# DLRM tower on one Trainium2 core: two tables' last rows fetched by SyncE, high parts of tables placed in PSUM, casts ahead, and another order of a group's work

## The chip, the cores and the metric

The kernel runs on one core of one Trainium2 chip. The time is the device time of that core in microseconds (us), the median of several runs. PE is the matrix engine (TensorE), DVE VectorE, ACT ScalarE, POOL GpSimd, SP SyncE; a q behind a name is that engine's sequencer. The span of a profile runs from the first instruction to the last, and the device time of the same execution is a little longer.

## The reference

For 2048 samples, 26 ids each pick one 128-wide row of 26 tables (nine of those with 1000 rows are called hot tables here; the other 17 have 1000 to 125000 rows). With the sample's dense row these are 27 vectors; their 351 pairwise dot products and the dense row go through a three-layer MLP.

```python
e = jnp.stack([tbl_0[ids[:, 0]], ..., tbl_25[ids[:, 25]]], axis=1)
combined = jnp.concatenate([dense[:, None, :], e], axis=1)           # 2048 x 27 x 128
inter = jnp.einsum('bnd,bmd->bnm', combined, combined)[:, triu_i, triu_j]
h = jnp.concatenate([dense, inter, dense], axis=1)                    # 607 wide
h = jnp.maximum(h @ W_top1 + b_top1, 0.0)                             # 512
h = jnp.maximum(h @ W_top2 + b_top2, 0.0)                             # 256
y = h @ W_top3                                                        # 1
```

## The kernel before

The batch is cut into 16 tiles of 128 samples; two tiles are a group (8 groups). Work is written as a list of steps per tile, and PE, ACT and DVE each walk the same list and do their own part of each step, in order. The lists are `FIRST_STEPS` (before group 0), `STEPS` (two lists, for the first and second tile of groups 0 to 6) and `LAST_STEPS` (group 7). A letter and a number are one step:

- Q, transposes: PE transposes the gathered rows of one bank of 3 or 4 tables of the **next** tile (L650) into `transpose_ps`; ACT (even n, L408) or DVE (odd n, L545) copies them to `embed_t`.
- H, look-up in a hot table for the **next** group: DVE makes a one-hot matrix of the ids (L538, reads ids that PE has broadcast into PSUM at L659, once for two look-ups), PE multiplies it with the table's high and low part (L684, 16 products), ACT copies the result (L461). Each one-hot is made two look-ups ahead, as soon as its slot of two is free. Even n use the bank `hot_ps`, odd n bank 1 of `mlp_ps`.
- G, gram: PE forms the dot products of 64 samples (L714, 128 records); ACT copies the late columns (L455), then DVE the early ones (L527, COPY_PREDICATED) into `units`.
- SP then stores a group's `units` to DRAM (`bounce`, L316), waits, and reads them back in another layout (L320). S of the **following** group is the split of what landed: ACT casts the high part (L449), DVE subtracts for the low part (L549).
- M0 to M3, M4 and M5, M6: the three layers of the MLP for the **previous** group (L720 to L722, 12 products each, and L761). M0 needs the low part of S. ACT applies the activation (L416, L420), DVE takes the low part (L569); M2 uses the bank of M0, and waits for M0's low part.
- D splits the group's dense rows (ACT L442, DVE L549); E copies dense rows into `embed_t`. W splits the MLP weights in group 0 alone.

POOL does one thing: 272 indirect gathers, 17 a tile (L390), each waiting that the same bank of two tiles earlier has been transposed. SP issues all other transfers from one queue, in order. Its loop over the groups is

```python
for g in range(GROUPS - 1):
    if g + 2 < GROUPS:
        load_dense(g + 2)          # waits for D of group g: its buffer is dense_sb[g % 2]
    pack(g, g % 2, packed_raw)     # bounce and read back
    if g >= 1:
        store_y(g - 1)
```

In the start, nine hot tables are loaded, ACT casts each to `table_hi` (L488, fp32r), and DVE subtracts this from the loaded table for `table_lo` (`split_lo`, L549).

Of the kernel before, what the change touches and what calls it, by code (L numbers as in the profile page):

```python
# [41 lines left out]
P = 128  # L42
TABLES = 26
N = TABLES + 1
B = 2048
# [22 lines left out]
PAIR_ROWS = HOT * GROUPS // PAIR  # L68
HALF = N // 2
# [27 lines left out]
    "G0 S0 Q0 H0 M0 Q1 Q2 H1 G1 W0 Q3 H2 W1 M1 Q4 M2 W2 H3 W3".split(),  # L97
    "G0 M3 Q0 H4 W4 M4 D0 E0 Q1 Q2 H5 W5 G1 Q3 H6 M5 Q4 H7 H8 M6".split(),
# [13 lines left out]
def dlrm_tower(nc, dense_t, ids, hot_ids, row_numbers, tables, w1_dense, w1_again, w1_units, b1, w2, b2, w3, identity, late_rows, bounce, y):  # L112
    ctx = ExitStack()
    with ctx:
# [24 lines left out]
        selector = sb("selector", [P, PAIR_ROWS], F32R)  # L139
# [14 lines left out]
        y_sb = sb("y_sb", [P, 2, GROUP], F32)  # L154

        def unit_p(c):

            return BIAS_P if c == 0 else UNIT_P

# [17 lines left out]
        stage_b = y_sb[:, :, :].rearrange("p i b -> p (i b)")  # L177
# [20 lines left out]
        selector_ready = sem("selector_ready")  # L198
        hot_ids_ready = sem("hot_ids_ready")
# [3 lines left out]
        banks_zeroed = sem("banks_zeroed")  # L203
# [50 lines left out]
        def dense_columns(g):  # L254

            return dense_group(g).rearrange("p (q s) -> p s q", s=BLOCK)

# [34 lines left out]
        def _(sp):  # L292
# [30 lines left out]
            def store_y(g):  # L323

                sp.wait_ge(mlp_copied, MLP_USES * (g + 1) + (g < GROUPS - 1))
                sp.dma_start(y[g * GROUP:(g + 1) * GROUP, :].rearrange("b c -> c b"), y_sb[0:1, g % 2, :]).then_inc(y_stored[g % 2], 16)
# [49 lines left out]
        def _(pool):  # L376
            def gather(tile):
# [6 lines left out]
                for u in range(TILE_BANKS):  # L384
# [3 lines left out]
                    for f in features(u):  # L388
                        table = GATHERED_TABLES[f - 1]
# [5 lines left out]
            nc.gpsimd.dma_start(hot_ids_sb[:, :], hot_ids).then_inc(hot_ids_loaded, 16)  # L395
# [8 lines left out]
        def _(act):  # L404
# [5 lines left out]
            def mlp_copy(g, buf, m):  # L410
# [6 lines left out]
                elif m < H1_CHUNKS + H2_CHUNKS:  # L417

                    c = m - H1_CHUNKS
                    nc.scalar.activation(hidden2[c].rearrange("p (q s) -> p s q", s=BLOCK),  # L420
                                         src.rearrange("p (s q) -> p s q", s=BLOCK),
                                         ACT.Relu, bias=b2_sb[:, c:c + 1]).then_inc(mlp_copied, 1)
                else:
                    if g >= 2:

                        act.wait_ge(y_stored[g % 2], 16 * (g // 2))
                    nc.scalar.copy(y_sb[0:1, g % 2, :], src[0:1, :]).then_inc(mlp_copied, 1)
# [93 lines left out]
        def _(dve):  # L521
# [78 lines left out]
            nc.vector.memset(gram_ps[:, :, :], 0.0).then_inc(banks_zeroed, 1)  # L600

            dve.wait_ge(const_loaded, 16 * 2)
            nc.vector.tensor_copy(selector[:, :], identity_sb[:, 0:PAIR_ROWS]).then_inc(selector_ready, 1)
# [32 lines left out]
        def _(pe):  # L636
# [4 lines left out]
            def transposes(g, buf, t2, u):  # L641
                tile = TILES * g + t2
                pe.wait_ge(gathered[t2][u], 16 * len(features(u)) * (g + 1))
# [5 lines left out]
                for i, f in enumerate(features(u)):  # L649
                    last = nc.tensor.transpose(transpose_ps[:, (t2 * TILE_BANKS + u) % 2, i, :], rows[:, t2, f - 1, :], identity_sb[:, :])  # L650
                last.then_inc(transposed, 1)

            def broadcast_ids(pair):

                if pair >= 1:
# [4 lines left out]
                                 selector[:, pair:pair + 1].to_broadcast([P, HOT_P]), hot_ids_sb[:, :],  # L660
                                 start=True, stop=True).then_inc(hot_ids_ready, 1)

# [165 lines left out]
            pe.wait_ge(hot_ids_loaded, 16)  # L828
            broadcast_ids(0)

# [79 lines left out]
```

## Time and profile before

| | us |
|---|---|
| median of 3 runs (381.84 to 385.08) | 384.82 |
| the profiled execution | 385.81 |
| its span | 383.9 |
| PE busy | 333.5 |
| POOL busy | 269.4 |
| DVE busy | 260.9 |
| ACT busy | 169.3 |

The busy time of POOL leaves out 0.30 us between two gathers, in which its sequencer issues the next one; the engine does nothing else in that time.

### The profile page before, as it was taken

The numbers are of one execution on the slowest core, as the hardware profiler recorded it, in microseconds if no ns is written. First come the engines' busy times: TensorE is split into PE (matmuls) and PEld (weight loads), VectorE is DVE, ScalarE is ACT, GpSimd is POOL, SyncE is SP. The second block draws the span as 40 slices with busy tenths as digits, with TensorE's granted clock in tenths as the row PEclk, the third lists the DMA queues.
The fourth block names the chain that finished last, engine by engine and source line by source line (L and its number), as shares of the span: only waits on it lengthen the run. The fifth ranks groups of instructions, "written<-read, shape, count | busy, mean of one in ns | idle before, by whom it ended". The sixth has DMA issues, their size and how long they took to land.

```text
span 383.9 us, 13545 instructions
## 1 busy us (share of the span) xinstructions
PE 333.5 (87%) x6208; PEld 303.5 (79%) x6208; DVE 260.9 (68%) x206; ACT 169.3 (44%) x248; POOL 269.4 (70%) x277
## 2 busy tenths in 40 slices
PE   3777895949899998999899989999898989969787
PEld 2656784939898897979898879889897889859676
DVE  3999889574849865787668775777666776723322
ACT  2553563514445443545364543544354434532412
POOL 6787777777777777777777777777777777776000
PEclk9999998797999999999999999999999999997999
DMA  7996124251224322242215221341224112332020
GB/s 181 234 236 188 51 70 112 57 158 50 56 55 118 88 58 56 66 144 52 56 51 158 51 57 54 94 121 50 56 66 143 51 50 58 97 99 56 2 92 0
DMA packets 18985, 33.51 MB, mean 87 GB/s; under 512 B 5834, under 2 KB 11666, under 8 KB 18930
## 3 DMA queue, kind: packets, MB, share of 16 engines
q0 software_dynamic: 8848, 18.11, 18.2%
q1 hardware_dynamic: 10082, 14.55, 13.5%
q8 instruction: 49, 0.80, 0.8%
q14 instruction: 6, 0.05, 0.0%
HBM read 28.96 MB, written 3.68 MB: 85 GB/s over the span
## 4 chain that ended last, share of the span: by engine, by line
PE 40%; POOL 34%; issue 13%; DVE 7%; DMA 3%; ACT 2%; DVEq 0%; SPq 0%
POOL rows L390 34%; PE gram_ps L714 8%; PE hot_ps L684 8%; PE mlp_ps L684 8%; PE mlp_ps L720 4%; DVE one_hot L538 3%; PE transpose_ps L650 3%; PE mlp_ps L721 3%; PE mlp_ps L722 3%; DVE units L527 2%; DMA rows<-table,ids_sb 1%; PE hot_ids_ps L659 1%; PE mlp_ps L761 1%; DMA rows<-bounce 1%; DVE packed_lo L549 1%
## 5 line engine op out<-in xcount | busy, mean ns | idle before, releaser
L390 POOL DMA_INDIRECT rows<-table,ids_sb x272 | 268.5, 987 | 83.5 <-issue 80.7
L538 DVE TENSOR_TENSOR one_hot<-hot_ids_ps,row_numbers_sb 125x2048 fp32r<-125x2048 f32 x72 | 165.2, 2298 | 72.2 <-PE hot_ids_ps L659 62.7
L684 PE MATMUL hot_ps<-one_hot,table_hi 125*128 125x256 f32 x320 | 82.5, 295 | 3.4 <-issue 2.9
L684 PE MATMUL hot_ps<-one_hot,table_lo 125*128 125x256 f32 x320 | 79.6, 286 | 0.0
L684 PE MATMUL mlp_ps<-one_hot,table_hi 125*128 125x256 f32 x256 | 66.6, 297 | 11.8 <-DVE hidden_lo L569 6.4
L684 PEld LDWEIGHTS hot_ps<-one_hot,table_hi 125*128 125x128 f32 x320 | 62.1, 194 | 4.6 <-issue 4.6
L714 PE MATMUL gram_ps<-embed_t 128*27 128x27 f32 x4096 | 54.9, 195 | 11.2 <-issue 4.8
L684 PE MATMUL mlp_ps<-one_hot,table_lo 125*128 125x256 f32 x256 | 63.8, 286 | 0.0
L714 PEld LDWEIGHTS gram_ps<-embed_t 128*27 128x27 f32 x4096 | 45.0, 106 | 23.0 <-issue 15.4
L684 PEld LDWEIGHTS hot_ps<-one_hot,table_lo 125*128 125x128 f32 x320 | 62.3, 195 | 0.1
L684 PEld LDWEIGHTS mlp_ps<-one_hot,table_hi 125*128 125x128 f32 x256 | 49.9, 195 | 14.6 <-DVE one_hot L538 7.4
L408 ACT COPY embed_t<-transpose_ps 128x512 f32<-128x512 f32 (+1 forms) x48 | 55.1, 1148 | 7.8 <-PE transpose_ps L650 7.6
L461 ACT COPY embed_t<-hot_ps 128x256 f32<-128x256 f32 x40 | 27.3, 683 | 53.6 <-PE hot_ps L684 53.6
L527 DVE COPY_PREDICATED units<-late_sb,gram_ps 128x208 f32<-128x208 int32 x32 | 35.2, 1101 | 22.2 <-ACT units L455 22.1
L650 PE MATMUL transpose_ps<-identity_sb,rows 128*128 128x128 f32 x272 | 43.3, 282 | 7.9 <-DMA rows<-table,ids_sb 7.9
L684 PEld LDWEIGHTS mlp_ps<-one_hot,table_lo 125*128 125x128 f32 x256 | 50.0, 195 | 0.0
L650 PEld LDWEIGHTS transpose_ps<-identity_sb,rows 128*128 128x128 f32 x272 | 31.9, 143 | 12.1 <-DMA rows<-table,ids_sb 9.8
L455 ACT COPY units<-gram_ps 128x224 f32<-128x224 f32 x32 | 17.9, 561 | 51.7 <-PE gram_ps L714 51.7
L461 ACT COPY embed_t<-mlp_ps 128x256 f32<-128x256 f32 x32 | 21.8, 682 | 36.7 <-PE mlp_ps L684 36.5
L545 DVE COPY embed_t<-transpose_ps 128x384 f32<-128x384 f32 x32 | 33.0, 1032 | 0.0
L720 PE MATMUL mlp_ps<-packed_hi,w1u_hi 126*128 126x256 f32 (+1 forms) x90 | 26.4, 294 | 3.8 <-DVE packed_lo L549 3.8
L721 PE MATMUL mlp_ps<-packed_lo,w1u_hi 126*128 126x256 f32 (+1 forms) x90 | 25.8, 286 | 0.0
(80 smaller groups left out, 381.4 us busy)
## 6 DMA issues: line engine op xcount, KB each, us to landing
rows<-table,ids_sb POOLq DMA_INDIRECT x272
embed_t<-table SPq DMA_DIRECT2D x8, 448.0 KB
bounce<-units SPq DMA_DIRECT2D x8, 448.0 KB, 2.6
scratch<-bounce SPq DMA_DIRECT2D x7, 378.0 KB
dense_sb<-dense_t SPq DMA_DIRECT2D x8, 128.0 KB
scratch<-w SPq DMA_DIRECT2D x1, 512.0 KB, 4.8
units<-w_units SPq DMA_DIRECT2D x2, 252.0 KB
scratch<-table SPq DMA_DIRECT2D x1, 448.0 KB
```

The source lines that it names most:

```text
L390: nc.gpsimd.indirect_dma_start(rows[:, t2, f - 1, :], None, tables[table], bass.IndirectOffsetOnAxis(ids_sb[:, tile, table:table + 1], 0)) ...
L408: nc.scalar.copy(embed_target(g, t2, u), embed_source(t2, u)).then_inc(even_copied, 1)
L455: nc.scalar.copy(unit_slot(buf, r, 0, UNITS), gram_slot(r, HALF, N)).then_inc(late_copied, 1)
L461: nc.scalar.copy(out, hot_bank(k).rearrange("p (t b) -> p t b", t=TILES)).then_inc(hot_copied, 1)
L527: nc.vector.copy_predicated(unit_slot(buf, r, 1, UNITS), rows_taken, gram_slot(r, 0, HALF)).then_inc(early_copied, 1)
L538: nc.vector.tensor_tensor(one_hot[:, k % RING], ids.to_broadcast([HOT_P, HOT_STEPS, GROUP]), row_numbers_sb[:, :, None].to_broadcast([HOT_ ...
L545: nc.vector.tensor_copy(embed_target(g, t2, u), embed_source(t2, u)).then_inc(odd_copied, 1)
L650: last = nc.tensor.transpose(transpose_ps[:, (t2 * TILE_BANKS + u) % 2, i, :], rows[:, t2, f - 1, :], identity_sb[:, :])
L684: last = nc.tensor.matmul(hot_bank(n), table[:, n, step, :], one_hot[:, k % RING, step, :], start=(step == 0 and table is table_hi), stop= ...
L714: last = nc.tensor.matmul(gram_ps[32 * s:32 * s + N, r % 2, q * N:(q + 1) * N], embed_t[:, slot, b, :], embed_t[:, slot, b, :], start=True ...
L720: nc.tensor.matmul(out, w[0], x[0], start=start, stop=False)
L721: nc.tensor.matmul(out, w[0], x[1], start=False, stop=False)
```

## The change

- **SP fetches rows.** The last two gathered tables of tile 15 are left out of POOL's gathers (270 instead of 272). SP reads their 256 ids into registers, 16 at a time, and issues one transfer of one row for each, in six portions (48, 48, 48, 48, 32, 32 rows) behind a group's `pack` and `store_y`. They land in `last_rows`, which takes the place of `y_sb`; y now leaves from row 0 of `hidden2_first`, and ACT waits for the store of y before it writes `hidden2_first` again.
- **High parts in PSUM.** PE multiplies `table_hi` with an identity into the two `gram_ps` banks (`place_hi`, two products of 512 columns), and `split_lo` reads the high part there instead of from SBUF. Each `place_hi` waits until the low part of the table before is done. The zeroing of `gram_ps` goes away, and the unused half of `hot_ids_sb` is zeroed by DVE instead of loaded.
- **Casts ahead.** ACT casts one hot table further ahead.
- **Order.** The two lists of `STEPS` are written anew. `FIRST_STEPS` and `LAST_STEPS` are as before.

```diff
 STEPS = [
-    "G0 S0 Q0 H0 M0 Q1 Q2 H1 G1 W0 Q3 H2 W1 M1 Q4 M2 W2 H3 W3".split(),
-    "G0 M3 Q0 H4 W4 M4 D0 E0 Q1 Q2 H5 W5 G1 Q3 H6 M5 Q4 H7 H8 M6".split(),
+    "G0 S0 Q0 H0 W0 H1 G1 Q1 W1 M0 M1 Q2 M2 H2 W2 Q3 H3 W3 Q4 M3 H4".split(),
+    "G0 Q0 H5 W4 M4 M5 G1 Q1 E0 Q2 H6 W5 H7 Q3 H8 Q4 D0 M6".split(),
 ]
...
+            def fetch_rows(loads):
+
+                for _ in range(loads):
+                    n, at = divmod(fetched["rows"], P)
+                    table = GATHERED_TABLES[GATHERED - SP_TABLES + n]
+                    with ExitStack() as held:
+                        numbers = [held.enter_context(sp.register(f"row{n}_{at + i}")) for i in range(SP_LOAD)]
+                        sp.load(numbers, last_ids[n:n + 1, at:at + SP_LOAD])
+                        for i, number in enumerate(numbers):
+                            row = sp.snap(number, min_val=0, max_val=ROWS[table] - 1)
+                            sp.dma_start(last_rows[at + i:at + i + 1, n, :], tables[table][bass.ds(row, 1), :]).then_inc(rows_fetched, 16)
+                    fetched["rows"] += SP_LOAD
...
                 if g >= 1:
                     store_y(g - 1)
+                if g < len(SP_LOADS):
+                    fetch_rows(SP_LOADS[g])
...
                     for f in features(u):
+                        if fetched_by_sp(tile, f):
+                            continue
...
             split_hi(0)
+            split_hi(1)
             for step, n in [(x[0], int(x[1:])) for x in FIRST_STEPS]:
                 if step == "H":
-                    if n + 1 < HOT:
-                        split_hi(n + 1)
+                    if n + 2 < HOT:
+                        split_hi(n + 2)
...
             def split_lo(k):
-                dve.wait_ge(hi_split, k + 1)
-                lower(raw_tables[k], table_hi[:, k], table_lo[:, k]).then_inc(lo_split, 1)
+                dve.wait_ge(hi_placed, k + 1)
+                nc.vector.tensor_tensor(in_banks(table_lo[:, k]), in_banks(raw_tables[k]), gram_ps[0:HOT_P, :, :],
+                                        ALU.subtract).then_inc(lo_split, 1)
...
+            def place_hi(k):
+
+
+                pe.wait_ge(hi_split, k + 1)
+                if k >= 1:
+
+                    pe.wait_ge(lo_split, k)
+                for a in range(2):
+                    last = nc.tensor.matmul(gram_ps[:, a, :], identity_r[0:HOT_P, :], in_banks(table_hi[:, k])[:, a, :],
+                                            start=True, stop=True)
+                last.then_inc(hi_placed, 1)
...
+            place_hi(0)
 
             for _ in range(FIRST_WARM_PRODUCTS):
...
                 if step == "H":
+                    if n + 1 < HOT:
+                        place_hi(n + 1)
                     look_up(0, n)
```

SP's queue around one `pack`, before: the stretch is one turn of the loop over the groups (g = 2). `dense_split_lo` is set by DVE's part of D, `early_copied` by DVE's part of the group's last G.

```order
L301 DMA dense_sb<-dense_t 128x256 [waits dense_split_lo,dense_placed]
L316 DMA bounce<-units 128x896 [waits early_copied]
L320 DMA scratch<-bounce 126x4x192 [waits units_stored]
L326 DMA y<-y_sb 1x256 [waits mlp_copied]
L301 DMA dense_sb<-dense_t 128x256 [waits dense_split_lo,dense_placed]
```

The same turn after the change, up to the first fetched row (47 more of them follow, with two more reads of ids):

```order
L315 DMA dense_sb<-dense_t 128x256 [waits dense_split_lo,dense_placed]
L330 DMA bounce<-units 128x896 [waits early_copied]
L334 DMA scratch<-bounce 126x4x192 [waits units_stored]
L340 DMA y<-hidden_first 1x256 [waits mlp_copied]
L351 TENSOR_LOAD last_ids_ptr
L351 REGISTER_ALU
L351 TENSOR_LOAD last_ids
L353 ISA
L354 DMA last_rows<-table 1x128
```

The order of the first three transfers is unchanged: the dense load, with its wait for D, stands ahead of the bounce.

DVE in the second tile of a group and into the next group, before, from D to the first low part of the MLP (COPY_PREDICATED is G, `dense_lo` is D, `packed_lo` is S, `hidden_lo` is the MLP's low part):

```order
L549 TENSOR_TENSOR dense_lo<-dense_sb,dense_hi 128x256 [waits dense_split_hi]
L545 COPY embed_t<-transpose_ps 128x3x128 [waits transposed]
L538 TENSOR_TENSOR one_hot<-hot_ids_ps,row_numbers_sb 125x2048 [waits hot_ids_ready,hot_ready]
L527 COPY_PREDICATED units<-late_sb,gram_ps 128x16x13 [waits late_copied]
L545 COPY embed_t<-transpose_ps 128x3x128 [waits transposed]
L538 TENSOR_TENSOR one_hot<-hot_ids_ps,row_numbers_sb 125x2048 [waits hot_ready]
L538 TENSOR_TENSOR one_hot<-hot_ids_ps,row_numbers_sb 125x2048 [waits hot_ids_ready,hot_ready]
L538 TENSOR_TENSOR one_hot<-hot_ids_ps,row_numbers_sb 125x2048 [waits hot_ready]
L527 COPY_PREDICATED units<-late_sb,gram_ps 128x16x13 [waits late_copied]
L549 TENSOR_TENSOR packed_lo<-scratch,packed_hi 126x768 [waits units_hi]
L538 TENSOR_TENSOR one_hot<-hot_ids_ps,row_numbers_sb 125x2048 [waits hot_ids_ready,hot_ready]
L569 SCALAR_TENSOR_TENSOR hidden_lo<-mlp_ps,hidden_hi 128x256 [waits mlp_copied]
```

The same boundary after the change:

```order
L573 TENSOR_TENSOR one_hot<-hot_ids_ps,row_numbers_sb 125x2048 [waits hot_ids_ready,hot_ready]
L584 TENSOR_TENSOR dense_lo<-dense_sb,dense_hi 128x256 [waits dense_split_hi]
L562 COPY_PREDICATED units<-late_sb,gram_ps 128x16x13 [waits late_copied]
L584 TENSOR_TENSOR packed_lo<-scratch,packed_hi 126x768 [waits units_hi]
L573 TENSOR_TENSOR one_hot<-hot_ids_ps,row_numbers_sb 125x2048 [waits hot_ready]
L573 TENSOR_TENSOR one_hot<-hot_ids_ps,row_numbers_sb 125x2048 [waits hot_ids_ready,hot_ready]
L562 COPY_PREDICATED units<-late_sb,gram_ps 128x16x13 [waits late_copied]
L580 COPY embed_t<-transpose_ps 128x3x128 [waits transposed]
L605 SCALAR_TENSOR_TENSOR hidden_lo<-mlp_ps,hidden_hi 128x256 [waits mlp_copied] x3
```

D has moved from the middle of the group's second tile to its end, next to S of the following group, and between S and the first `hidden_lo` there now stand two one-hots, a G and a copy where one one-hot stood.

## Rows read from the trace of the kernel before

**Rows 1.** The page: the span.

```profile
span 383.9 us, 13545 instructions
```

**Rows 2.** POOL's waits: releaser, total us, times, longest us.

```profile
POOL rows L390 <- issue: 80.7, 265, 0.3
```

**Rows 3.** Timeline of PE: start us, us, instruction [idle before].

```profile
83.02 1.25 PE L714 MATMUL gram_ps<-embed_t 128*27 128x27 f32 x103 [1.06 <-ACT embed_t L461]
...
128.63 1.91 PE L714 MATMUL gram_ps<-embed_t 128*27 128x27 f32 x128
...
212.14 1.88 PE L714 MATMUL gram_ps<-embed_t 128*27 128x27 f32 x128
...
334.09 0.66 PE L650 MATMUL transpose_ps<-identity_sb,rows 128*128 128x128 f32 x4 [0.50 <-DMA rows<-table,ids_sb]
...
339.74 1.73 PE L714 MATMUL gram_ps<-embed_t 128*27 128x27 f32 x118
```

**Rows 4.** PE's waits from 90 to 335 us.

```profile
PE mlp_ps L684 <- DVE hidden_lo L569: 6.4, 6, 1.3
PE transpose_ps L650 <- DMA rows<-table,ids_sb: 2.2, 4, 1.3
PE mlp_ps L684 <- ACT scratch L420: 1.8, 4, 0.6
```

**Rows 5.** Timeline of POOL and DVE around one table's low part, and the last gather.

```profile
12.83 1.21 DVE L549 TENSOR_TENSOR table_lo<-embed_t,table_hi 125x1024 fp32r<-125x1024 f32 x1
13.09 1.78 POOL L390 DMA_INDIRECT rows<-table,ids_sb  x1 [0.30 <-issue]
...
352.99 0.94 POOL L390 DMA_INDIRECT rows<-table,ids_sb  x1 [0.30 <-issue]
```

**Rows 6.** The chain that ended last: one look-up's 16 products.

```profile
336.76 1.92 PE hot_ps L684 x16
```

**Rows 7.** Timeline of SP and of the ACT cast behind the last pack.

```profile
200.54 0.36 SPq L301 DMA_DIRECT2D dense_sb<-dense_t  x1
204.47 0.34 SPq L316 DMA_DIRECT2D bounce<-units  x1
...
366.26 0.35 SPq L316 DMA_DIRECT2D bounce<-units  x1
...
372.19 1.02 ACT L515 CAST packed_hi<-rows 126x256 fp32r<-126x256 f32 x3 [6.50 <-DMA rows<-bounce]
```

**Rows 8.** Timeline of ACT, DVE and PE at a G, S and M0.

```profile
182.29 1.09 DVE L527 COPY_PREDICATED units<-late_sb,gram_ps 128x208 f32<-128x208 int32 x1
183.00 1.19 DVE L545 COPY embed_t<-transpose_ps 128x384 f32<-128x384 f32 x1
...
215.03 0.86 ACT L449 CAST packed_hi<-scratch 126x768 fp32r<-126x768 f32 x1
...
215.99 1.17 DVE L549 TENSOR_TENSOR packed_lo<-scratch,packed_hi 126x768 fp32r<-126x768 f32 x1
...
217.09 2.27 DVE L538 TENSOR_TENSOR one_hot<-hot_ids_ps,row_numbers_sb 125x2048 fp32r<-125x2048 f32 x1
...
217.22 0.39 PE L720 MATMUL mlp_ps<-packed_hi,w1u_hi 127*128 127x256 f32 x1 [0.47 <-DVE packed_lo L549]
...
218.40 0.93 PE L650 MATMUL transpose_ps<-identity_sb,rows 128*128 128x128 f32 x7
...
219.28 0.41 DVE L569 SCALAR_TENSOR_TENSOR hidden_lo<-mlp_ps,hidden_hi 128x256 fp32r<-128x256 f32 x1
```

**Rows 9.** Stretches: PE, PEld, DVE, ACT, POOL busy, granted clock, DMA.

```profile
344.40:351.20 6.80, 5.52 (x143) 5.03 (x144) 2.48 (x4) 1.54 (x3) 5.28 (x6) 0.50 0.22 58
```

**Rows 10.** Timeline of PE in group 7, where no pack is late.

```profile
342.84 0.27 PE L714 MATMUL gram_ps<-embed_t 128*27 128x27 f32 x10 [1.37 <-issue]
...
345.68 0.58 PE L720 MATMUL mlp_ps<-packed_hi,w1u_hi 127*128 127x256 f32 x1 [1.75 <-DVE packed_lo L549]
...
359.39 1.27 PE L714 MATMUL gram_ps<-embed_t 128*27 128x27 f32 x128 [1.37 <-ACT embed_t L408]
```

More of the change, by code:

```diff
@@ L68 @@
 PAIR_ROWS = HOT * GROUPS // PAIR
+HOT_IDS_P = 64
+SP_TABLES = 2
+SP_LOAD = 16
+SP_LOADS = [3, 3, 3, 3, 2, 2]
 HALF = N // 2
@@ L109, with dlrm_tower @@
 FIRST_STEPS = "H0 Q0 H1 Q1 H2 H3 Q2 H4 H5 Q3 H6 H7 Q4 E0 H8".split()
-def dlrm_tower(nc, dense_t, ids, hot_ids, row_numbers, tables, w1_dense, w1_again, w1_units, b1, w2, b2, w3, identity, late_rows, bounce, y):
+def dlrm_tower(nc, dense_t, ids, hot_ids, last_ids, row_numbers, tables, w1_dense, w1_again, w1_units, b1, w2, b2, w3, identity, late_rows, bounce, y):
     ctx = ExitStack()
@@ L153, in dlrm_tower, with fetched_by_sp @@
         hidden2_first = sb("hidden2_first", [P, GROUP], F32)
-        y_sb = sb("y_sb", [P, 2, GROUP], F32)
+        last_rows = sb("last_rows", [P, 2 * SP_TABLES, P], F32)
         def unit_p(c):
             return BIAS_P if c == 0 else UNIT_P
+        def fetched_by_sp(tile, f):
+            return tile == TILE_COUNT - 1 and f > GATHERED - SP_TABLES
         def by_chunk(at):
@@ L256, in dense_columns, with in_banks @@
             return dense_group(g).rearrange("p (q s) -> p s q", s=BLOCK)
+        def in_banks(table):
+            return table.rearrange("p (a j) d -> p a (j d)", a=2)
         def gram_slot(i, first, last):
@@ L419, in mlp_copy @@
                     c = m - H1_CHUNKS
+                    if c == 0 and g >= 1:
+                        act.wait_ge(y_stored[(g - 1) % 2], 16 * ((g + 1) // 2))
                     nc.scalar.activation(hidden2[c].rearrange("p (q s) -> p s q", s=BLOCK),
@@ L423, in mlp_copy @@
                 else:
[L424 to L427 removed]
+                    nc.scalar.copy(hidden2_first[0:1, :], src[0:1, :]).then_inc(mlp_copied, 1)
             def dense_place(g):
@@ L642, in transposes @@
                 tile = TILES * g + t2
-                pe.wait_ge(gathered[t2][u], 16 * len(features(u)) * (g + 1))
+                others = sum(fetched_by_sp(tile, f) for f in features(u))
+                pe.wait_ge(gathered[t2][u], 16 * (len(features(u)) * (g + 1) - others))
+                if others:
+                    pe.wait_ge(rows_fetched, 16 * SP_TABLES * P)
                 if u >= 2:
@@ L649, in transposes @@
                 for i, f in enumerate(features(u)):
-                    last = nc.tensor.transpose(transpose_ps[:, (t2 * TILE_BANKS + u) % 2, i, :], rows[:, t2, f - 1, :], identity_sb[:, :])
+                    source = last_rows[:, f - 1 - GATHERED + SP_TABLES, :] if fetched_by_sp(tile, f) else rows[:, t2, f - 1, :]
+                    last = nc.tensor.transpose(transpose_ps[:, (t2 * TILE_BANKS + u) % 2, i, :], source, identity_sb[:, :])
                 last.then_inc(transposed, 1)
@@ L890 @@
         late[:, k:k + HALF, k - 1] = 1
-    hot_ids = np.zeros((P, PAIR * GROUP), np.int32)
+    last_ids = np.ascontiguousarray(a["ids"][B - P:, GATHERED_TABLES[GATHERED - SP_TABLES:]].T)
+    hot_ids = np.zeros((HOT_IDS_P, PAIR * GROUP), np.int32)
     hot_ids[:PAIR_ROWS] = a["ids"].T[HOT_TABLES].reshape(HOT, GROUPS, GROUP).transpose(1, 0, 2).reshape(PAIR_ROWS, PAIR * GROUP)
```

25 lines of the change are left out of this document (14 added, 11 removed).

## Prediction

> **What bounds the kernel now.** I read POOL's waits first. In 265 of 272 gathers it waited for nothing but its own issue time, 0.30 us each [rows 2], so POOL runs without a stop from the start to its last gather at 352.99 us [rows 5]. The timeline of PE then tells how close PE runs behind it. Take the first G of each even tile as a mark: tile 2 at 83.02, tile 4 at 128.63, tile 8 at 212.14, tile 14 at 339.74 [rows 3]. Between tiles 4 and 8 a group takes (212.14 - 128.63) / 2 = 41.8 us. POOL needs 34 x 1.25 = 42.5 us for a group, plus lengthened gathers. So PE is the faster by a little, comes up to POOL late in the run, and waits for it there: the transposes at 334.09 waited for rows [rows 3], and over 90 to 335 us such waits sum to only 2.2 us [rows 4]. From the mark at 339.74 to the end of the span (383.9 [rows 1]) are 44.2 us of PE work and of the last pack. Two chains nearly tied: a gain on POOL counts only if PE can follow.
>
> **Gathers left to SP.** Two gathers fewer end POOL 2.5 us sooner in tile 15. It helps nothing by itself: the last bank of tile 15 was transposed behind queued MLP products, just before the G at 359.39 [rows 10], and the last rows had landed by about 355.5 (352.99 plus the 2.5 us from issue to landing that separates 331.59 from 334.09). SP pays. One transfer costs its queue 0.34 to 0.36 us with 128 partitions [rows 7]; taking that for one row, 48 rows are 17 us a group, and even 0.8 us each would be 38, inside a group. The transfers stand behind pack and store_y, so what they could delay is the next turn's dense load, a group later. I take 0, and +5 us at worst. The reads of ids have no row. The Trainium skill ("DMA: Bandwidth & Descriptors", on hardware figures) has a floor of about 600 ns for a tensor_load; by that three reads would add 1.8 us to the 17, which changes nothing.
>
> **High parts in PSUM.** While DVE takes a table's low part from two SBUF operands (1.21 us at 12.83), the gather that overlaps it takes 1.78 us instead of 0.94 [rows 5]; the one-hots of 2.3 us, one operand in PSUM, lengthen none. There are eight lengthened gathers up to 40 us, five by 0.84 and three by 0.16 to 0.33: 5.0 us in all. With the high part read from PSUM I expect them gone and every gather from 40 us on 5.0 us earlier. The price is PE's: 18 products, and at the start `place_hi(0)` waits for ACT's cast and the eight warm-up products now stand behind it, so the first look-up and DVE's chain of one-hots start 2 us later. DVE bounds the start before and after, so group 0 begins 2 us later. The zeroing, the halved load of ids and the cast ahead lie off this chain: 0.
>
> **Group 0, new order.** PE has no MLP there. From tile 0's mark to tile 2's took 40.6 us before, of which 3.9 us were a wait for rows that now land 5 us earlier, and some 3 us a half clock behind it. DVE's list is about 28 us up to the last one-hot of the group, PE's own work about 31. I take 34 us from a start at 44.5: tile 2's mark at 78 instead of 83.0. Bounds: 76 and 82.
>
> **A middle group, new order.** What is removed: PE's waits of H3 behind M2 and of H7 behind M5, (6.4 + 1.8) / 5.9 groups = 1.4 us a group by idle time [rows 4], about 1.8 start to start. So a group without waits is 41.8 - 1.8 = 40.0 us. What is added comes from D. SP's dense load waits for D and stands ahead of the bounce. Before, D was in mid-tile, the load went out at 200.54 and the bounce at 204.47, when G was done, not D [rows 7]; the rows were back before the next group began. Now D is the last step but one. Let 0 be PE's first G of the next group. That G waits for ACT's copy of Q4, and ACT casts D right behind that copy, then DVE subtracts: D is done at +1.1, or at +2.0 in every second group, where DVE's one-hot ahead of D first needs an id broadcast. The bounce goes out 0.4 later, and from a bounce to ACT's start on the rows it reads back took 372.19 - 366.26 = 5.93 us [rows 7]; in mid-run, with gathers beside it, I take 6.2. ACT's S so starts at a = +7.7 (or +8.6).
>
> From there, start to start [rows 8]: DVE's S at a + 0.96, the next instruction 1.10 later, and M0's products on the landed rows at a + 2.2. DVE was blocked at S and must then make two one-hots (2.19 each, 217.09 to 219.28), G's copy (0.71, 182.29 to 183.00), Q1's copy (0.75 taken alike), and only then M0's low part (0.41), all of which stand ahead of it in its queue: done at a + 0.96 + 1.10 + 4.38 + 0.71 + 0.75 + 0.41 = a + 8.3. M2 writes over M0's bank and waits for it: +16.1, and +17.6 in the other groups, where the broadcast of the second one-hot's ids waits for the first (0.7 more). Without waits M2 would start at two G (1.9 each), two H (1.92 [rows 6]), Q0 to Q2 (1.0), M0 and M1 (1.4 each, nine products in 1.18 us [rows 8]) and a broadcast (0.2): +11.7. So this costs 4.4 or 5.9, mean 5.1 us. Smaller: G for Q4's copy 0.2, M3 for H3's copy 0.4, H8 right behind H7 0.2. A group is then 40.0 + 5.9 = 45.9 us, against 41.8. Its bounds: below, 42.9, if only M0's own lateness (1 to 2 us) counts and DVE's queue does not; above, 47.
>
> **The clock.** Three times the granted clock of PE fell to half for 6.8 us, as in 344.40 to 351.20 [rows 9] (the two levels are 1.2 and 2.4 GHz). Ahead of that one stood gaps of 1.37 and 1.75 us with a little work between [rows 10]; ahead of another a single gap of 3.9. The new order has in each of six groups a gap of 3 to 4 us and a shorter one. I expect a fall in four of the six, each worth 3.4 us less what of it lies in the gap, 2.4: 9.6 us. Bounds 0 and 17. The Trainium skill ("TensorE: Matmul & The Clock Gate", part 1) ties the low level to an idle stretch of PE; read strictly, gaps cut up by work would not bring it, and the result is the rival "no falls" below. The fall at 344.40 came behind a cut-up gap, so this trace leans the other way.
>
> **Sum.** Tile 2 at 78; six groups of 45.9 are 275.4 (the packs of groups 0 to 5 stand behind a dense load; that of group 6 does not, so the last group is as before): tile 14 at 353.4. Plus 44.2: 397.6. Plus 9.6: span 407.2. The profiled execution was 1.9 over its span (385.81), the median 384.82 0.9 over it; with 0.9: **408 us**, 6% slower. POOL, 5 us ahead, is no bound any more.
>
> **Rivals.** (1) No falls of the clock: 397.6 + 0.9 = 398.5. For it: group 0's idle pieces of 1 to 2 us bring none. (2) The other side: S's lateness does not reach PE, because the pack is quicker or D done sooner than I have it. Then POOL bounds: tile 14's last rows land at 334.05 - 5.0 = 329.05, the transposes take 0.4, ACT's copy 1.64 more before G (H7 and H8, 3.8 us, no longer stand between), tile 14's mark at 331.1 and the end at 375.3, device 376. It decides where a group stays under (331.1 - 78) / 6 = 42.2 us; the point of no change is (339.7 - 78) / 6 = 43.6. What speaks against it: it needs under 2.2 us of waits, and S alone lands at +7.7. (3) DVE's queue is not what M2 waits for, and a group is 42.9: mark at 335.4, then 380.5, device 381 to 386 with a fall or two: no change. (4) SP's rows take over 0.85 us each and push the dense load beyond D: 3 to 5 us more a group, 420 or over.
>
> **How the numbers follow.** Slower with falls 0.47, without 0.27, SP overrun 0.03; faster 0.17; no change 0.06. A difference of 1% is about what a measurement of this kernel can tell. Case (3) lies partly on either side of that bound, so: faster 0.18, same 0.08, slower 0.74. The slow cases' own range is 392 to 420. To leave out no more than 2 in 10 I cut off most of the faster case and the overrun: 384 to 422.
>
> **What would show it.** Marks of tile 2 at 76 to 82 and then 45 to 49 us apart; the bounce 0.4 us behind each dense load, both about 1 us into the next group; ACT's S at +7.7; DVE idle 4 to 5 us ahead of `packed_lo`; PE idle at M2 for `hidden_lo`; half clock in most middle groups; no gather lengthened before 40 us; POOL waiting for transposes late in the run, since PE falls behind it. I am wrong if `packed_lo` does not wait, or if M2 starts before +13.

## The result, and the profile after

The changed kernel took **415.86 us** (median of 4 runs, 411.40 to 419.58) against 384.73 us for the kernel before on the same chip. The ratio is 1.0781, 95% interval 1.0685 to 1.0877: 8% slower. Ratios here and below leave out runs in which the chip was in a slower state, so they are not quite the quotient of the medians beside them. The profiled execution took 417.02 us, 1.8 over its span.

The page of the changed kernel: the span, the granted clock of PE in 40 slices (9 is full speed), and the chain that ended last.

```profile
span 415.2 us, 14406 instructions
...
PEclk9999999997999779998999969999899969998989
...
PE 47%; DVE 31%; DMA 14%; ACT 4%; issue 3%; SPq 1%; DVEq 0%
```

POOL held 34% of the chain before and has no share of it now; DVE's one-hots and the two transfers of a pack have taken its place. The marks (PE's first G of an even tile, which answer to [rows 3]):

```profile
79.57 0.63 PE L767 MATMUL gram_ps<-embed_t 128*27 128x27 f32 x47 [1.48 <-ACT embed_t L441]
...
129.62 0.56 PE L767 MATMUL gram_ps<-embed_t 128*27 128x27 f32 x44 [0.16 <-ACT embed_t L441]
...
179.89 0.29 PE L767 MATMUL gram_ps<-embed_t 128*27 128x27 f32 x13 [0.37 <-ACT embed_t L441]
...
370.65 0.53 PE L767 MATMUL gram_ps<-embed_t 128*27 128x27 f32 x40 [0.37 <-ACT embed_t L441]
```

Three stretches hold the account: tile 2 is reached 3.5 us sooner than before, the six middle groups take (370.65 - 79.57) / 6 = 48.5 us each, and the end is 44.6 us long as it was (44.2). Stretches of the changed kernel (columns as in [rows 9]):

```profile
0.00:79.57 79.57, 62.15 (x888) 55.02 (x889) 68.04 (x49) 36.56 (x49) 59.35 (x66) 1.00 0.53 140
79.57:370.65 291.08, 248.97 (x4622) 229.41 (x4622) 180.04 (x137) 112.70 (x174) 200.01 (x210) 0.94 0.26 73
370.65:415.20 44.55, 34.34 (x717) 31.30 (x717) 13.26 (x21) 14.00 (x27) 0.00 (x0) 0.92 0.06 21
```

and the same middle stretch of the kernel before:

```profile
83.02:339.74 256.72, 239.58 (x4622) 219.78 (x4623) 179.25 (x137) 118.11 (x174) 195.47 (x202) 0.99 0.27 76
```

The same 4622 products keep PE busy 9.4 us longer (249.0 against 239.6: the clock), and PE stands idle 42.1 us (291.1 - 249.0) instead of 17.1. So the loss is 25.0 us of waits and 9.4 of clock in the middle groups. Whose waits, the list of waits of the changed kernel says (us in total, times, longest):

```profile
ACT packed_hi L483 <- DMA scratch<-bounce: 44.4, 6, 8.7
DVE packed_lo L584 <- ACT packed_hi L483: 42.8, 6, 8.4
...
PE hot_ids_ps L700 <- DVE one_hot L573: 18.6, 5, 7.3
POOL rows L423 <- PE transpose_ps L691: 15.8, 15, 2.8
...
PE mlp_ps L773 <- DVE packed_lo L584: 12.0, 5, 4.2
...
PE mlp_ps L773 <- DVE hidden_lo L605: 7.1, 3, 3.3
```

Six times, once for each middle group, ACT stands at S for the packed rows, DVE for ACT, and then PE for DVE. PE's part reaches it at three places: an id broadcast that waits for a one-hot, M0's products on the landed rows, and M2. POOL, for 15.8 us, waits for PE: it is no bound. One such place from its start, SP's queue of the changed kernel:

```profile
131.50 0.37 SPq L315 DMA_DIRECT2D dense_sb<-dense_t  x1
131.93 0.44 SPq L330 DMA_DIRECT2D bounce<-units  x1
135.55 0.35 SPq L334 DMA_DIRECT2D scratch<-bounce  x1
...
140.18 26.80 SPq L354 DMA_DIRECT2D last_rows<-table  x48
182.15 0.37 SPq L315 DMA_DIRECT2D dense_sb<-dense_t  x1
182.58 0.43 SPq L330 DMA_DIRECT2D bounce<-units  x1
185.79 0.35 SPq L334 DMA_DIRECT2D scratch<-bounce  x1
```

The bounce goes out 0.43 us behind the dense load, 2.3 us after the group's mark of 129.62, where before it went out in the group that made its rows [rows 7]. ACT and DVE of the changed kernel behind it:

```profile
140.73 0.83 ACT L483 CAST packed_hi<-scratch 126x768 fp32r<-126x768 f32 x1 [8.68 <-DMA scratch<-bounce]
```

```profile
130.82 0.61 DVE L584 TENSOR_TENSOR dense_lo<-dense_sb,dense_hi 128x256 fp32r<-128x256 f32 x1
...
141.59 0.96 DVE L584 TENSOR_TENSOR packed_lo<-scratch,packed_hi 126x768 fp32r<-126x768 f32 x1 [8.41 <-ACT packed_hi L483]
142.47 2.28 DVE L573 TENSOR_TENSOR one_hot<-hot_ids_ps,row_numbers_sb 125x2048 fp32r<-125x2048 f32 x1
145.71 2.29 DVE L573 TENSOR_TENSOR one_hot<-hot_ids_ps,row_numbers_sb 125x2048 fp32r<-125x2048 f32 x1 [0.95 <-PE hot_ids_ps L700]
```

D is done at 131.43, and the dense load that waited for it goes out at 131.50. S starts 11.1 us into the group, and DVE has done nothing for 8.41 us although a one-hot stood right behind. The chain of work that ended last runs through this place:

```profile
131.93 3.61 DMA bounce<-units
135.55 5.16 DMA scratch<-bounce
140.73 0.84 ACT packed_hi L483
141.59 0.96 DVE packed_lo L584
```

PE in two neighbouring groups of the changed kernel:

```profile
144.81 0.79 PE L700 MATMUL hot_ids_ps<-hot_ids_sb,identity_r 128*125 128x512 f32 x1 [7.31 <-DVE one_hot L573]
...
191.85 0.58 PE L773 MATMUL mlp_ps<-packed_hi,w1u_hi 127*128 127x256 f32 x1 [3.04 <-DVE packed_lo L584]
...
198.34 0.36 PE L773 MATMUL mlp_ps<-dense_hi,w1d_hi 128*128 128x256 f32 x1 [2.01 <-DVE hidden_lo L605]
```

In the first, the broadcast of ids waits 7.3 us for the one-hot that is queued behind S; in the second, with the broadcast ahead of H1, the same lateness comes out as 3.0 us at M0's landed products and 2.0 at M2. In the first, the granted clock falls to its lower level inside the gap and stays there behind it:

```profile
140.00:147.00 7.00, 2.19 (x9) 2.01 (x10) 4.45 (x3) 3.04 (x5) 5.48 (x6) 0.51 0.23 62
```

### The profile page after: what moved, and what is told of

It is laid out like the page before. It is cut to its first block, busy times and chain, and to the rows that moved or that the text cites. A ratio compares the mean times of both kernels' runs of the same rounds, so it can differ in the third digit from the quotient of the medians.

```text
span 415.2 us, 14406 instructions
## 1 busy us (share of the span) xinstructions
PE 345.5 (83%) x6226; PEld 315.7 (76%) x6226; DVE 261.3 (63%) x206; ACT 163.3 (39%) x248; POOL 259.4 (62%) x275
## 4 chain that ended last, share of the span: by engine, by line
PE 47%; DVE 31%; DMA 14%; ACT 4%; issue 3%; SPq 1%; DVEq 0%
DVE one_hot L573 21%; PE hot_ps L737 10%; PE gram_ps L767 7%; PE mlp_ps L737 6%; DMA scratch<-bounce 6%; DMA bounce<-units 6%; PE mlp_ps L773 6%; PE mlp_ps L774 5%; PE mlp_ps L775 5%; PE transpose_ps L691 4%; DVE embed_t L580 3%; DVE units L562 2%; PE hot_ids_ps L700 2%; DVE table_lo L588 1%; ACT packed_hi L483 1%
## 5 line engine op out<-in xcount | busy, mean ns | idle before, releaser
L423 POOL DMA_INDIRECT rows<-table,ids_sb x270 | 258.4, 957 | 94.1 <-issue 77.4
L737 PE MATMUL hot_ps<-one_hot,table_hi 125*128 125x256 f32 x320 | 81.1, 291 | 1.0 <-DVE one_hot L573 0.6
L737 PE MATMUL mlp_ps<-one_hot,table_hi 125*128 125x256 f32 x256 | 63.5, 287 | 0.0
L737 PE MATMUL mlp_ps<-one_hot,table_lo 125*128 125x256 f32 x256 | 62.6, 283 | 0.0
L767 PE MATMUL gram_ps<-embed_t 128*27 128x27 f32 x4096 | 52.8, 194 | 10.2 <-ACT embed_t L441 4.3
L737 PEld LDWEIGHTS mlp_ps<-one_hot,table_lo 125*128 125x128 f32 x256 | 49.0, 191 | 0.6
L737 PEld LDWEIGHTS mlp_ps<-one_hot,table_hi 125*128 125x128 f32 x256 | 49.0, 191 | 0.2
L773 PE MATMUL mlp_ps<-packed_hi,w1u_hi 126*128 126x256 f32 (+1 forms) x90 | 29.5, 328 | 12.0 <-DVE packed_lo L584 12.0
L700 PE MATMUL hot_ids_ps<-hot_ids_sb,identity_r 128*125 128x512 f32 x36 | 17.5, 486 | 23.6 <-DVE one_hot L573 18.6
L584 DVE TENSOR_TENSOR packed_lo<-scratch,packed_hi 126x768 fp32r<-126x768 f32 x7 | 6.9, 992 | 42.8 <-ACT packed_hi L483 42.8
```

The costliest lines, as they stand in the source:

```text
L423: nc.gpsimd.indirect_dma_start(rows[:, t2, f - 1, :], None, tables[table], bass.IndirectOffsetOnAxis(ids_sb[:, tile, table:table + 1], 0)) ...
L700: nc.tensor.matmul(hot_ids_ps[0:HOT_P, :], identity_r[:, pair:pair + 1].to_broadcast([P, HOT_P]), hot_ids_sb[:, :], start=True, stop=True) ...
L737: last = nc.tensor.matmul(hot_bank(n), table[:, n, step, :], one_hot[:, k % RING, step, :], start=(step == 0 and table is table_hi), stop= ...
L767: last = nc.tensor.matmul(gram_ps[32 * s:32 * s + N, r % 2, q * N:(q + 1) * N], embed_t[:, slot, b, :], embed_t[:, slot, b, :], start=True ...
L773: nc.tensor.matmul(out, w[0], x[0], start=start, stop=False)
```

## Experiments

Twelve runs. Two of the sets landed on chips on which the kernel before took 551.05 and 550.50 us instead of 385: there PE, ACT and DVE stood idle again and again with no semaphore to explain it. Their times can only be read as ratios to the kernel before on that chip, and I repeated what mattered. Ratios are given with their 95% interval.

### The pack ahead of the dense load: pack_first, pack_first_2

```diff
-                if g + 2 < GROUPS:
-                    load_dense(g + 2)
                 pack(g, g % 2, packed_raw)
+                if g + 2 < GROUPS:
+                    load_dense(g + 2)
```

> The changed kernel with two statements of SyncE's loop exchanged: the pack of a group (bounce and read) now stands ahead of the dense load that waits for D. Theory A (D, moved to a group's end, holds up the pack through SyncE's queue): the bounce goes out when the last G of a group is done, about 5 us ahead of D, the rows are back before ACT comes to S, ACT's wait ahead of packed_hi falls from 8.7 us to under 1, DVE's ahead of packed_lo as well, and the marks stand 41 to 42.5 us apart instead of 48.5. POOL is then the bound again: tile 14's mark at about 331 to 336, the end 44 later, so 377 (374 to 383). Rival B (SyncE's row transfers clog the queue or the DMA engines): the marks stay 46 to 49 apart and the time over 400. Rival C (the order of the MLP steps and look-ups costs by itself): the bounce is early but a group still takes 44 or more, 392 to 405.

Measured on a 551 us chip: 538.88 us where before took 551.05, 0.9825 (0.9722 to 0.9928). The time can't be set against the expected 377; as a ratio that was 0.98. It doesn't decide either: on that chip the new order with its late pack had 0.9755 (order_alone, below).

> The same kernel as pack_first (the changed kernel with the pack ahead of the dense load in SyncE's loop), once more, because in the first call the kernel before took 551 us where it had taken 385, with gaps of 0.7 to 9 us that all engines' instruction streams show and that hide waits of a few us. Theory A (D through SyncE's queue holds up the pack): if the kernel before is near 385 us here, ACT waits under 1 us ahead of packed_hi and a group takes 41 to 42.5 us, 377 (374 to 383). Rival B (row transfers) or C (the order by itself): 392 or more.

Measured: **381.09 us** against 385.73, 0.9882 (0.9829 to 0.9936). Two statements exchanged give back all of the loss and 1.2% more. SP's queue of this kernel, at the place that answers to 131.50 above:

```profile
154.34 0.36 SPq L330 DMA_DIRECT2D bounce<-units  x1
156.96 0.33 SPq L334 DMA_DIRECT2D scratch<-bounce  x1
164.22 0.36 SPq L315 DMA_DIRECT2D dense_sb<-dense_t  x1
...
168.09 26.42 SPq L354 DMA_DIRECT2D last_rows<-table  x48
```

The bounce leaves 7.6 us ahead of the next mark (161.96), the dense load still waits for D, and nothing that is needed soon stands behind it. ACT's wait ahead of S is down to 0.3 us once in the run. Tile 14 is at 331.23, inside the expected 331 to 336. The middle of the run and that mark's transposes of this kernel:

```profile
78.70:331.23 252.53, 237.55 (x4622) 218.23 (x4622) 179.50 (x137) 115.11 (x174) 191.82 (x200) 1.00 0.29 80
```

```profile
329.32 0.66 PE L691 MATMUL transpose_ps<-identity_sb,rows 128*128 128x128 f32 x4 [1.13 <-DMA rows<-table,ids_sb]
```

Groups take 42.1 us and the clock does not fall in them. The 1.13 us at 329.32 are PE's one listed wait for POOL's rows in the six groups, so POOL bounds this run only at its end. The expected 377 was missed by 4: the tail took 378.7 - 331.2 = 47.5 us, not 44. Its PE is busy for 36.7 us at a clock of 0.89 (34.5 before), and it waits 0.7 and 0.4 us for the rows of tile 15's last two banks (345.55 and 347.95), which had long landed in the changed kernel, where PE came to them late. Rivals B and C fall: the fetch and the order are unchanged here.

### D back in mid-tile: d_mid, d_mid_2

```diff
-    "G0 Q0 H5 W4 M4 M5 G1 Q1 E0 Q2 H6 W5 H7 Q3 H8 Q4 D0 M6".split(),
+    "G0 Q0 H5 W4 M4 M5 D0 G1 Q1 E0 Q2 H6 W5 H7 Q3 H8 Q4 M6".split(),
```

> The changed kernel with one step moved in LAST_STEPS: D0 stands between M5 and G1 of a group's second tile instead of ahead of the last M6. SyncE's loop is as in the changed kernel (dense load ahead of the pack). Theory A (what costs is D's place before the pack): D is done some 10 us ahead of the last G, the dense load goes out early, the bounce as soon as G is done, and the marks are 41 to 43 apart, 378 (375 to 385). Rival B (row transfers): over 400. Rival C (the rest of the order costs): groups of 44 or more, 392 to 405.

The step was moved in `STEPS`, as the diff shows; the expectation names the wrong list.

Measured on the 551 us chip: 532.22 us, 0.9712 (0.9587 to 0.9836).

> The kernel of d_mid once more, on a chip where the kernel before takes its 385 us: the changed kernel with D0 moved from the end of a group to between M5 and G1 of its second tile; dense load still ahead of the pack. Theory A (D holds up the pack through SyncE's queue): marks 41 to 43 us apart, ACT's wait ahead of packed_hi under 1 us, 378 (375 to 385). Rival B (row transfers) over 400, rival C (the rest of the order) 392 to 405.

Measured: **381.66 us** against 385.36, 0.9915 (0.9884 to 0.9946). SP's order of statements is the changed kernel's; only D is done earlier. SP's queue of this kernel:

```profile
196.73 0.37 SPq L315 DMA_DIRECT2D dense_sb<-dense_t  x1
198.94 0.35 SPq L330 DMA_DIRECT2D bounce<-units  x1
201.52 0.35 SPq L334 DMA_DIRECT2D scratch<-bounce  x1
```

The bounce is out 7.4 us ahead of the next mark (206.33). ACT waits for packed rows once, for 2.3 us (under 1 was expected), in all other groups for nothing that is listed. Two different edits, one on SP and one on ACT and DVE, break the same link and give the same time. So it is the link (D, dense load, pack) that costs, not D's place as such, nor the order of SP's loop.

### The old order with everything else: old_order, old_order_2

Both lists of steps are those of the kernel before; fetch, placing and casts ahead stay.

> The changed kernel with both lists of steps of the kernel before put back; SyncE's fetch, the high parts in PSUM and the casts ahead stay. Theory A: those parts cost nothing in the middle groups; group 0 starts 2 us later but its rows land earlier; marks 41.8 apart, tile 14's mark 334 to 338, end 44 later: 380 (376 to 384), at or a little below the kernel before. Rival B (the row transfers or the placing are what made the change slow): over 400, with marks 46 or more apart.

Measured on the 551 us chip: 555.61 us, 1.0104 (0.9978 to 1.0230).

> The kernel of old_order once more: the changed kernel with both lists of steps of the kernel before; SyncE's fetch, the high parts in PSUM and the casts ahead stay. Theory A: 48 rows a group in SyncE's queue cost nothing, the bounce goes out when G is done, marks 41.8 apart, 380 (376 to 385). Rival B (the row transfers need the early pack of the new SyncE loop as well, since they sit right ahead of the next dense load): a dense load later than in the kernel before and 388 or more.

Measured: **383.29 us** against 385.36, 0.9946 (0.9925 to 0.9967). The parts besides the order gain 2 us. Tile 2 is reached at 80.77 (83.02 before), tile 14 at 335.78 (339.74), and 46.5 us remain instead of 44.2. The rows do sit right ahead of the dense load, which goes out as soon as the last of them has, and it is in time:

```profile
169.24 26.39 SPq L354 DMA_DIRECT2D last_rows<-table  x48
195.73 0.37 SPq L315 DMA_DIRECT2D dense_sb<-dense_t  x1
199.09 0.35 SPq L330 DMA_DIRECT2D bounce<-units  x1
```

### The new order alone: order_alone, order_alone_2

The kernel before with the changed kernel's two lists of steps and nothing else.

> The kernel before with only the two lists of steps of the changed kernel: POOL gathers all rows and the high parts stay in SBUF. Theory A (the order is the whole loss): groups of 48 to 48.5 us, ACT waiting 7 to 9 us ahead of packed_hi in each of six groups; tile 2's mark a few us later than in the changed kernel since the first gathers are lengthened: 415 (410 to 420). Rival B (SyncE's 48 row transfers per group are needed for the loss): 385 to 395.

Measured on the 551 us chip: 536.01 us, 0.9755 (0.9633 to 0.9878). There the new order is a gain. ACT's waits for the packed rows sum to 18.6 us there (40.0 in order_alone_2), and pack_first and d_mid, without a late pack, are not clearly faster. So on these chips none of the three prices the link. Of this more below.

> The kernel of order_alone once more: the kernel before with only the two lists of steps of the changed kernel; POOL gathers all rows, high parts stay in SBUF. Theory A: the order alone gives the whole loss: ACT waits 7 to 9 us ahead of packed_hi in six groups, marks 48 to 49 apart, tile 2's mark a few us later than in the changed kernel because gathers are lengthened at the start: 416 (410 to 422). Rival B (the 256 row transfers are needed for the loss, by making the packs slower): 385 to 400.

Measured: **412.38 us** against 385.36, 1.0716 (1.0675 to 1.0756). Waits and middle stretch of this kernel:

```profile
ACT packed_hi L449 <- DMA scratch<-bounce: 40.0, 6, 7.7
```

```profile
77.51:366.45 288.94, 249.66 (x4622) 229.89 (x4622) 180.06 (x137) 112.62 (x174) 207.66 (x218) 0.93 0.27 75
```

Without one row transfer on SP and without a product for placing, the middle groups take 48.2 us (48.5 with them), PE is idle for 39.3 us over the six and the clock is at 0.93. The order gives all of the loss that can be told apart: 3.5 us lie between this median and that of the changed kernel, and the interval overlaps with that of 1.0781 (1.0685 to 1.0877). Tile 2 is reached at 77.51, where the expectation had it a few us later than in the changed kernel (79.57): 2.1 us earlier, although the gathers at the start are lengthened here.

### No fetch: no_fetch

pack_first with `SP_LOADS = []` and `fetched_by_sp` returning False: POOL gathers all 34 tables.

> The kernel of pack_first with SyncE's fetch of the last tile's two tables taken out: POOL gathers all 34 tables of every group. If SyncE's fetch is worth what it takes off POOL: pack_first was held by POOL's rows at tile 14 (PE waited 1.4 us ahead of tile 14's last bank) and by tile 15's banks (0.98 and 0.71 us), so two gathers more, at the end of tile 15, add 2.5 us to the last rows: 1 to 2.5 us slower than pack_first, 382 to 384. If the 256 row transfers disturb gathers and packs (POOL's gathers have a mean of 968 ns with them, 957 in the changed kernel): the same as pack_first or 1 to 2 us faster.

Measured: 382.86 us against 385.36, 0.9942 (0.9916 to 0.9967); pack_first_2 had 0.9882 (0.9829 to 0.9936). The difference of 1.8 us has the sign and size of the first case, but the intervals overlap a little and the two did not run in one set: by the ratios the fetch is worth anything from nothing to some 5 us once the pack is early. Tile 14's mark is the same, 331.20; the difference lies behind it.

### One step moved in the kernel before: d_last_alone

```diff
-    "G0 M3 Q0 H4 W4 M4 D0 E0 Q1 Q2 H5 W5 G1 Q3 H6 M5 Q4 H7 H8 M6".split(),
+    "G0 M3 Q0 H4 W4 M4 E0 Q1 Q2 H5 W5 G1 Q3 H6 M5 Q4 H7 H8 D0 M6".split(),
```

> The kernel before with one step moved: D0 from between M4 and E0 of a group's second tile to behind H8, ahead of M6. Nothing else differs. Theory A (dense load waiting for D stands ahead of the pack in SyncE's queue): ACT waits 6 to 8 us ahead of packed_hi in six groups, and in this order M0's products on the landed rows stand at +4.5 us from a group's start instead of +9 as in the changed kernel, so PE waits there for about 7 to 8 us: groups of 49 to 51.5 us, slower than the changed kernel: 430 (420 to 440). Rival (the loss needs the new places of M0, M2 and the look-ups): 384 to 392.

Measured: 598.22 us where before took 550.50, **1.1004** (1.0917 to 1.1092). The expectation's range was 1.09 to 1.14 of 385, so in ratio it holds. The waits of this kernel stand where they were expected (ACT's are 8.1 us on average, against 6 to 8):

```profile
ACT packed_hi L449 <- DMA scratch<-bounce: 48.6, 6, 10.0
...
223.69 0.58 PE L720 MATMUL mlp_ps<-packed_hi,w1u_hi 127*128 127x256 f32 x1 [7.90 <-DVE packed_lo L549]
```

D's place alone, with every other step where it was, delays the pack and stops PE for 7.9 us at M0. The idle time at G that no semaphore explains is 95.8 us here, no more than the 102.8 us of old_order, which has no late pack and had 1.0104; so the 10% are not its doing, as far as two chips can be compared. The absolute time on a 385 us chip was not measured.

### New order and early pack without fetch and placing: order_pack_first

The kernel before with the new lists of steps and the exchange of pack_first.

> The kernel before with the changed kernel's two lists of steps and the pack ahead of the dense load in SyncE's loop; no fetch by SyncE, no high parts in PSUM. Against no_fetch (382.9 us), which has the high parts in PSUM too, it prices them. If the gathers lengthened at the start are on the path (POOL is the bound at tile 14): its rows come about 4 us later than in no_fetch, tile 14's mark at 334 to 336 instead of 331.2, 385 to 387. If they are not, and PE's later start with the placed parts counts instead: 382 or less.

Measured on the 550 us chip: 532.79 us, 0.9771 (0.9707 to 0.9835). It was to be set beside no_fetch, which ran on a 385 us chip, and can't be. The nearest is pack_first on the other 551 us chip, 0.9825 (0.9722 to 0.9928): nothing there speaks for a gain from placing. The order with the late pack had 0.9755 (0.9633 to 0.9878) on a chip of this kind, the same as with the early pack here. What the placed parts are worth with an early pack stays open.

### S later in the queues: s_late

```diff
-    "G0 S0 Q0 H0 W0 H1 G1 Q1 W1 M0 M1 Q2 M2 H2 W2 Q3 H3 W3 Q4 M3 H4".split(),
+    "G0 Q0 H0 W0 H1 G1 Q1 W1 S0 M0 M1 Q2 M2 H2 W2 Q3 H3 W3 Q4 M3 H4".split(),
```

> The changed kernel with S0 moved in STEPS from behind G0 to just ahead of M0; the pack stays late. ACT and DVE then make their copies and DVE its two one-hots before they come to the late rows. Theory A with its middle link (a blocked DVE and ACT queue passes the lateness on to the id broadcast and to M2): PE waits only at M0's products on the landed rows, from about +8.8 to +12.5 us, 4 us a group instead of 6.4: groups of 45.5 to 46.5, with one or two falls of the clock less, 400 (394 to 406). Rival (only the time at which the rows land counts, whatever stands behind S): groups stay at 48 and the time at 411 to 418.

Measured on the 550 us chip: 557.94 us, 1.0257 (1.0171 to 1.0343). PE's waits of this kernel:

```profile
PE mlp_ps L773 <- DVE packed_lo L584: 24.6, 8, 4.3
PE hot_ids_ps L700 <- DVE one_hot L573: 12.3, 8, 2.6
```

The waits moved as the middle link says: up to 4.3 us at M0's landed products, no more 7 us at the broadcast, and at M2 PE went through. But the time does not decide. The changed kernel itself was not run on such a chip, and order_alone, whose S also comes late, had 0.9755 there: in groups that are so much longer ACT waits 18.6 us for the rows (40.0 on a 385 us chip), which may be why S moved back gains nothing in s_late; no run shows it. So the experiment shows where the waits go and not what the blocked queue is worth.

### What was different on the 551 us chips

PE inside one G of order_alone, 128 products that take 1.1 to 1.9 us elsewhere:

```profile
257.19 0.77 PE L714 MATMUL gram_ps<-embed_t 128*27 128x27 f32 x46 [7.79 <-ACT embed_t L408]
258.25 0.28 PE L714 MATMUL gram_ps<-embed_t 128*27 128x27 f32 x3 [0.28 <-issue]
258.98 0.34 PE L714 MATMUL gram_ps<-embed_t 128*27 128x27 f32 x5 [0.46 <-issue]
```

After some 46 products (16 and 40 in two G of old_order) it stands still again and again, here for 0.3 to 0.5 us, and waits for nothing that the trace shows. In order_alone such idle time at G is 46.0 us in 78 pieces, in old_order 102.8 us in 131, in the changed kernel on its own chip 1.6 us in 2. That goes with the new order being 2.5% faster there than the kernel before, while old_order's 1.0104 is not clear of noise: order_alone's second G of a tile ran in 1.1 us without a hole (207.25 to 208.39), where two of old_order's took 10.3 us each (216.06 to 226.4, 249.08 to 259.4). Why the new order has fewer holes is open. That instructions arrive late is what the pattern looks like; no run here shows the supply itself.

## Why the prediction was right

The forecast was 408 us with a range of 384 to 422; 415.9 lies in it, on the side and by the mechanism that the prediction took as likeliest. That it comes within 8 us is luck in part: two terms are off by 12.5 and by 8.3 us, with opposite signs. Its sum against the measured spans, with pack_first_2 as the new order without a late pack:

| term | predicted | measured | difference |
|---|---|---|---|
| tile 2's mark | 78.0 | 79.6 | +1.6 |
| six groups of the new order, pack in time (pack_first_2) | 6 x 40.0 = 240.0 | 252.5 | +12.5 |
| waits that the late pack adds | 6 x 5.9 = 35.4 | 42.1 - 15.0 = 27.1 idle | -8.3 |
| clock | 9.6 | 249.0 - 237.6 = 11.4 busy | +1.8 |
| from tile 14's mark on | 44.2 | 44.6 | +0.4 |
| span | 407.2 | 415.2 | +8.0 |

**The link from D to S was right, its length too short.** Shown, not only argued: break it at SP (pack_first) or at D (d_mid) and the loss is gone; make it in the kernel before (d_last_alone) and the loss is there. In the two groups above D was done at +1.8 and +2.2 (I had +2.0 and +1.1) and the bounce left 0.4 behind the dense load. But from the bounce to S's start passed 8.8 and 7.4 us where I took 6.2, from a last pack that had no dense load directly ahead of it [rows 7]. Part of that is in the trace: the read of the bounce follows it by 3.6 and 3.2 us here and by 3.4 in order_alone_2, with 0.4 us between dense load and bounce, and by 2.6, 2.6 and 2.9 in pack_first_2, d_mid_2 and old_order_2, with the dense load 2.2 us or more away. The nearness of the dense load can't be all of it: two packs of no_fetch took 3.5 and 3.6 us and one of pack_first_2 3.2 without one. The larger part lies behind the read: 5.2 and 4.2 us to the start of S, where 3.4 passed behind the last pack. What slows it is open. S so started at +11.1 and +10.1, not at +8.6 and +7.7 (at +9.5 to +10.1 in the last three of the six groups).

**What stands behind S.** M2 started at +21.5 and +18.5, where I had +17.6 and +16.1; counted from S that is 10.4 and 8.4, against my 9.0 and 8.4; M0's low part was done 9.3 and 8.2 us behind S's start, against my 9.0 and 8.3. So the chain of two one-hots and two copies was sized well. But I named M2 as the place where PE stands, and in every second group that was wrong: there M2 did not wait for that low part at all. PE stood 7.3, 4.7 and 4.8 us at the broadcast of ids, which I had only as 0.7 us on top of the other, and then ran M0 and M1 at half clock.

**The group without a late pack was mis-sized.** I took the old order's 41.8 and subtracted waits of 1.8 us. The new order has other ones: in pack_first_2 M2 still waits 0.9 to 1.4 us in every second group, with the pack in time, for a hidden_lo that stands behind the one-hots in DVE's queue. This was the step that failed: a group of 40.0 us would leave PE 240.0 - 237.6 = 2.4 us idle in all six, and it was idle for 15.0. POOL explains little of it: its rows held PE for 1.1 us of the 15.0, and d_mid_2, where no wait for rows is listed and POOL has no share of the chain that ended last, takes 253.5 us for the same six groups. The two errors cancelled for the most part.

**Rival (2), faster, was the right one for the wrong kernel.** It gave 376 for a pack that does not reach PE, and 331.1 for tile 14's mark. pack_first_2, where the pack does not, had 331.23 and 381.1. PE was only 1.1 us from being the bound itself there. The tail is 47.5 us long instead of the 44.2 that I carried over.

**The clock.** I expected falls in four of six groups; the granted clock fell to half in all six, 11.4 us of longer busy time in place of 9.6. Six of the seven falls come at or behind one unbroken gap of 3 us or more (7.31 ahead of 144.81, clock 0.51 from 140 to 147; 3.04 ahead of 191.85). The seventh, at 99 us in the first group, came behind a gap of only 1.83 us (ahead of 98.93), and in the tail one came at 375 us behind 1.73 (ahead of 374.49); the same length ahead of 287.37, 1.80 us, brought none. With gaps of up to 1.5 us pack_first_2 has none in its middle stretch, d_mid_2 one (at 252 us, behind 1.4 us). My rival of no falls rested on gaps cut up by work; most were not cut up. The Trainium skill ("TensorE: Matmul & The Clock Gate", part 1) ties the low level to an idle stretch; six falls of this trace agree, and those at 99 and 375 us speak against reading it strictly.

**SP's fetch cost nothing that shows, as predicted,** though 48 rows took 26.80 us where I had 17. The first 16 of them, behind one read of ids, show why:

```profile
140.18 6.88 SPq L354 DMA_DIRECT2D last_rows<-table  x16
```

That is 0.43 us a row, near the 0.35 that I took from wide transfers. The rest is the reads of ids, which the sum had at nothing because no row showed one: each is two loads of 1.18 and 1.77 us (medians), 3.0 us together, three to a portion of 48, where the estimate beside the sum had 1.8 us for all three. All in all 31 us fit into a group. Rival (4) did not come, and with the rows a middle group takes 48.5 us, without them and without placing 48.2 (order_alone_2).

**The start.** Group 0 began 1.4 us later, at 43.8 (I had 2 us and 44.5), and took 35.8 us instead of 34; my sum also rounded 44.5 + 34 = 78.5 down to 78.

**High parts in PSUM.** As predicted, no gather ahead of 50 us was lengthened in the changed kernel, and POOL was done with its early work sooner. Whether this brings tile 2's mark forward depends on the order: with the old one it does (80.8 with them in old_order_2, 83.0 without), with the new one it doesn't (79.6 in the changed kernel, 77.5 in order_alone_2). The traces show why. The later start costs 1.3 and 1.6 us at tile 0's mark. With the old order it is won back, since PE's wait of 3.9 us for rows in group 0 is gone in old_order_2; the new order has no such wait there even without the placed parts. No run takes the placing apart from the fetch and the casts. All parts besides the order together gained 2 us with the old order.

## What to carry to other kernels

A queue that issues transfers in order hands on every wait: before moving a step, list what waits for it in each queue and what stands behind that wait, and put transfers that something waits for soon ahead of those that wait for something late. Where a long list of edits loses, the loss can be one link; exchanging two statements turned 8% slower into 1% faster. A chain of waits sized from one quiet place of the trace can be too short in mid-run, here by 1.2 to 2.6 us of 6.2, and a group "without its waits" has others that stood behind them.

## What was not expected of the hardware

- A pack (448 KB out, 378 KB back) right behind a dense load of 128 KB always took long: 3.2 to 3.7 us from bounce to read in all twelve of the changed kernel and order_alone_2. Without one, packs of groups 0 to 6 mostly took 2.5 to 2.9, but two of no_fetch 3.5 and 3.6, so the dense load is not the only cause.
- SP issues a row transfer whose row number is read from a register every 0.43 us, against 0.34 to 0.36 us of queue time for a wide one; getting 16 such numbers into registers costs it 3.0 us more.
- One kernel took 385 us on some chips and 551 on others with identical instructions, and the order of the steps had the opposite sign there: 0.9755 against 1.0716 for order_alone.
